# Delta-rule loop on one core: ACT copies the turned gated output ahead of squares and Relu, SP loads the value weights a slot ahead and the 16-blocks a slot later

## What is computed

```python
y = silu(causal_conv4(concat(q, k, v)))            # q, k: 16 heads, v: 32 heads
beta = sigmoid(b); g = -exp(A_log) * softplus(a + dt_bias)
q, k = l2norm(q) * DK ** -0.5, l2norm(k)
def step(S, inp):                                  # for every token
    S = S * exp(gt)[:, None, None]
    delta = (vt - einsum('hk,hkv->hv', kt, S)) * bt[:, None]
    S = S + kt[:, :, None] * delta[:, None, :]
    return S, einsum('hk,hkv->hv', qt, S)
gated = core * silu(z)
gated = gated * rsqrt(mean(gated * gated, -1) + EPS) * norm_w
out = gated.reshape(B, T, VDIM) @ W_out
```

## Time and profile before

| | |
|---|---|
| median of 3 runs | 3170.8 us (3170.05 to 3171.24) |
| the profiled execution | 3182.26 us |
| its span, first to last instruction | 3180.4 us |
| mean granted clock of TensorE | 0.974 of full speed |
| busy: PE, DVE, ACT, POOL | 92%, 71%, 62%, 48% |
| the loop's full part | about 380 to 2760 us, one slot 18.94 us |

### The profile page before, as it was taken

One profiled execution on the slowest core, in us unless ns is written; L12 is line 12 of the kernel. 1 busy time (PEld: TensorE's weight loads), 2 busy tenths in 40 slices (PEclk: granted clock), 3 DMA queues, 4 the chain that ended last, 5 costly groups with the idle time before them and its releaser, 6 DMA issues. The chain is left out here.

```text
span 3180.4 us, 70682 instructions
## 1 busy us (share of the span) xinstructions
PE 2911.2 (92%) x22765; PEld 2132.7 (67%) x22765; DVE 2258.0 (71%) x4805; ACT 1956.3 (62%) x6436; POOL 1520.6 (48%) x3616
## 2 busy tenths in 40 slices
PE   5998599999999999999999999999999999978998
PEld 4555377677767776777677767777777777764655
DVE  3432577777777777777777777777777777745766
ACT  4322577677767776777677767776777777633332
POOL 2000466656655565666666656665566666610000
PEclk8999799999999999999999999999999999978999
DMA  3001222222222222222222222222222222200000
GB/s 83 1 1 23 45 56 49 56 51 65 54 55 53 57 53 53 53 56 57 50 56 51 57 50 61 57 60 50 60 50 56 50 58 50 46 14 30 7 7 14
DMA packets 482417, 147.42 MB, mean 46 GB/s; under 512 B 352592, under 2 KB 481216, under 8 KB 482048
## 3 DMA queue, kind: packets, MB, share of 16 engines
q1 hardware_dynamic: 482048, 142.81, 20.7%
HBM read 97.40 MB, written 45.35 MB: 45 GB/s over the span
## 5 line engine op out<-in xcount | busy, mean ns | idle before, releaser
L920 ACT ACTIVATE raw<-bank 128x512 f32<-128x512 f32 x256 | 153.3, 599 | 388.0 <-PE bank L680 382.5
L748 PE MATMUL bank<-wout_h,gT 128*128 128x256 f32 x1024 | 258.4, 396 | 114.2 <-ACT gT L948 114.2
L475 POOL TENSOR_TENSOR Tb<-Tb,btmp 64x14 f32<-64x14 f32 (+6 forms) x896 | 281.4, 314 | 70.1
L748 PEld LDWEIGHTS bank<-wout_h,gT 128*128 128x128 f32 x1024 | 186.2, 192 | 184.7 <-ACT gT L948 164.1
L471 POOL TENSOR_TENSOR btmp<-Bk,Tb 64x14 f32<-64x14 f32 (+6 forms) x896 | 253.7, 283 | 65.6
L459 POOL TENSOR_SCALAR Tb<-Bk 64x256 f32<-64x256 f32 x64 | 70.8, 1106 | 447.1 <-issue 414.2
L680 PE MATMUL bank<-xnT,wv 128*128 128x512 f32 x512 | 259.5, 631 | 23.7 <-DMA cv<-in_L_attn_conv_w_dram 16.1
L1191 DVE SCALAR_TENSOR_TENSOR conv<-raw,ckq,conv 128x512 f32<-128x512 f32 x384 | 262.1, 751 | 20.7 <-ACT conv L921 18.7
L1191 DVE SCALAR_TENSOR_TENSOR conv<-raw,cv,conv 128x512 f32<-128x512 f32 x384 | 265.5, 757 | 7.4 <-ACT conv L921 5.4
L680 PE MATMUL bank<-xnT,wkq 128*128 128x512 f32 x512 | 254.3, 621 | 17.2 <-POOL mkX L376 7.2
L850 ACT ACTIVATE sq_kq<-bank 128x128 bf16<-128x128 f32 x512 | 134.7, 278 | 185.1 <-PE bank L633 185.1
(11 more groups left out here) (352 smaller groups left out, 7639.3 us busy)
## 6 DMA issues: line engine op xcount, KB each, us to landing
rowb<-decay_rows SPq DMA_DIRECT2D x128, 256.0 KB, 5.2
blk_n<-N SPq DMA_DIRECT2D x128, 256.0 KB, 2.9
Tp<-blk_t SPq DMA_DIRECT2D x128, 128.0 KB, 2.9
Wp<-blk_w SPq DMA_DIRECT2D x128, 128.0 KB, 3.1
wkq<-in_L_attn_W_qkvz_dram SPq DMA_DIRECT2D x32, 128.0 KB, 4.3
wv<-in_L_attn_W_qkvz_dram SPq DMA_DIRECT2D x16, 256.0 KB, 4.9
Bk<-blk_n SPq DMA_DIRECT2D x64, 64.0 KB, 2.7
blk_t<-Tb SPq DMA_DIRECT2D x64, 64.0 KB, 2.5
```

The lines of the kernel that those rows point to most:

```text
L475: pool.tensor_tensor(Tb[:, j + 1:, 0:j], Tb[:, j + 1:, 0:j], tmp, ALU.subtract).then_inc(row_rdy, 1)
L748: i = pe.matmul(bB[0][:, h], gT[:, 2 * h + v, :], wout[:, v, :], start=(v == 0), stop=(v == 1))
L920: act.activation(raw[h][:, j, :, 3:], bB[1 - j], ACT.Copy)
```

## The change

ACT: in `body` the three calls `clamp`, `squares`, `gtev` become `gtev`, `squares`, `clamp`.

SP: the load of wv and cv leaves `weights` for a function `value_weights`, which takes the step one ahead of the newest, so that it is issued in the slot of the head's chunk 0. The load of Bk leaves `dump` for `base_load`, which takes the step at S_F + 1, so it is issued in the slot behind the one in which N was stored. The body becomes `decays`, `weights`, `base_load`, `value_weights`, `base_out`, `dump`. Waits of the loads are the same; POOL, PE and DVE are unchanged.

```diff
-                    if t.c == 1 and not first:
-                        free = held(sp, t.at(1, -1))
-                        sp.wait_ge(m["made"], 2)
-                        wait(sp, y_rdy, free)
-                        h = bass.ds(t.head(), 1)
-                        sp.dma_start(wv[:], wq[:, :, h, 2 * P:4 * P]).then_inc(wv_in, 16)
-                        sp.dma_start(cv[:], cw[:, bass.ds(t.head(2, 2 * HK), 2), :]).then_inc(wv_in, 16)
...
+                def value_weights(s):
+
+
+                    t = s.back(S_P - 1)
+                    if not t.live or t.c != 1 or (t.i is None and t.off < C):
+                        return
+                    free = held(sp, t.at(1, -1))
+                    sp.wait_ge(m["made"], 2)
+                    wait(sp, y_rdy, free)
+                    h = bass.ds(t.head(), 1)
+                    sp.dma_start(wv[:], wq[:, :, h, 2 * P:4 * P]).then_inc(wv_in, 16)
+                    sp.dma_start(cv[:], cw[:, bass.ds(t.head(2, 2 * HK), 2), :]).then_inc(wv_in, 16)
...
-                    made, read, sent, free = (held(sp, v) for v in (t.done(), t.pairs(16), t.at(16, 16), t.pairs()))
+                    made, read = held(sp, t.done()), held(sp, t.pairs(16))
...
-                    if t.c % 2:
-                        sp.wait_ge(m["made"], 2)
-                        wait(sp, n_out, sent)
-                        wait(sp, base_rdy, free)
-                        sp.dma_start(Bk[:], blocks(nd)).then_inc(blk_in, 16)
+
+                def base_load(s):
+
+                    t = s.back(S_F + 1)
+                    if not t.live or t.c % 2 == 0:
+                        return
+                    sent, free = held(sp, t.at(16, 16)), held(sp, t.pairs())
+                    sp.wait_ge(m["made"], 2)
+                    wait(sp, n_out, sent)
+                    wait(sp, base_rdy, free)
+                    sp.dma_start(Bk[:], blocks(nd)).then_inc(blk_in, 16)
 
                 def body(s):
                     decays(s)
                     weights(s)
+                    base_load(s)
+                    value_weights(s)
                     base_out(s)
                     dump(s)
...
                     evac(s, 1)
+                    gtev(s)
+                    squares(s)
                     clamp(s)
-                    squares(s)
-                    gtev(s)
                     expo(s)
```

## The result

| | before | after |
|---|---|---|
| median | 3170.8 us (3170.1 to 3171.2, 4 runs) | 3644.8 us (3636.7 to 3651.1, 4 runs) |
| ratio to before | 1 | 1.149, 95% interval 1.147 to 1.152 |
| span of the profiled execution | 3180.4 us | 3634.8 us |
| mean granted clock of TensorE | 0.974 | 0.912 |

The change costs 474 us by the medians, 454 by the profiled executions. The forecast was 3699 us, with a range of 3540 to 3880. I read the waits of each engine first. The four blocks, one each for PE, POOL, ACT and DVE, show for the loop's full part (400 to 3200 us) after the change who waited for whom: total us, times, longest.

A forecast was written before the change was run, and what follows sets the result against it. The prediction took TensorE to bound the kernel; the moved Bk load's 527 us plus 33 at heads' starts less 32 for value weights gave +528, so 3182.3 + 528 − 11.5 = 3699 us, range 3540 to 3880.

The forecast's parts named there:

- What bounds: TensorE bounds the loop, 37.9 us a pair; POOL's wait for Bk is no slack, a 12.4 us chain follows it.
- The order on SP: Bk's load issues 0.8 us behind Exp's end, behind the row load; 2.2 us later in 15 pairs, +33 us.
- Landing: Bk's load behind the row load lands in 4.3 us (2.7 to 5.3); POOL starts 5.2 us behind Exp's end.
- POOL: POOL from Bk to L408's end: 12.36 us less 0.8 (0 to 1.5), ending 16.8 us behind Exp's end.
- The stop: TensorE idles some 8 us ahead of solve, which starts 14.7 us behind Exp's end; apply follows at 18.8.
- The way back: From B's apply to the next A's: 18.94 less 0.93 for gT plus 0.5 for the clock, 18.5 us.
- The value weights: Issuing wv and cv a slot earlier removes 16.1 us of TensorE waits and 1.55 in each of 10: −32 us.
- Sum: Whole kernel: 62 pairs at +8.5 us, 527, plus 33 at heads, less 32 for value weights: +528 us; 80%.
- That POOL's wait takes the later load in: Rival: POOL's 6.9 us idle ahead of L459 absorbs the later Bk load, both wins stay: 3027 us, 5%.
- That the stall is half as long: Rival: VectorE and ACT catch up more, half the excess, +4 us a pair: 3420 to 3540 us, 6%.
- That SP passes the row load: Rival: Bk's load moves less, as if SP could pass the row load; loss and gain cancel: 3171 us, 2%.
- That the half clock outlives its time: Rival: TensorE's half clock outlives its 5.2 us behind the stop, some 4 us more a pair: 3950 us, 7%.

The follow-up runs named there:

- section 2: The change with Bk's load ahead of the row load in SP's next slot body: 3089.2 us, ratio 0.975 to the kernel before.
- section 3: The change with Bk's load at its old place, weights ahead of the row load, squares ahead of gT: 3061.9 us, ratio 0.966 to before.

## Why the prediction was right, step by step

The direction, the place and the size held. By its own steps:

- **What bounds.** That POOL's idle time ahead of L459 is no slack, but a wait with a chain of 12.4 us without a hole behind it, is what decided. The load ahead of the row load, in section 2, shows it from one side, the waits for N in section 3 from the other.
- **The order on SP.** Bk's load was to stand 0.6 us behind the row load and 0.8 behind Exp's end. Measured 0.56 and 0.79. At a head's start the row load went out at 1909.13 and Bk's at 1911.96: 2.27 later than elsewhere, forecast 2.2. A to B was 1.9 us longer there, in the mean.

```profile
1909.13 0.37 SPq L297 DMA_DIRECT2D rowb<-decay_rows  x1
...
1911.96 0.59 SPq L363 DMA_DIRECT2D Bk<-blk_n  x1
```

- **Landing.** I took 4.3 from wkq's row and bounds of 2.7 and 5.3. The median is 4.7, and POOL started at +5.7 in place of +5.2. The row load landed 5.1 behind its issue, so 4.5 behind Bk's. The Trainium skill's rule of ring order (DMA: Bandwidth & Descriptors, Queues, rings and completion order) has Bk's completion come no sooner than that of the row load, on every DMA engine that both use: the trace agrees, 0.2 us behind it by the medians. The sum went by wkq's row, 4.3, and that was 0.4 short.
- **POOL.** From Bk to the end of L408 I had 11.6. It was 9.83 (1869.21 to 1879.04), so the step was mis-sized by 1.7. The chain no longer ran beside VectorE's convolution, and its instructions ran at their short times, as L456 (L442 before) 0.19 for 0.65 and L489 0.28 for 0.62 on the same 64x50. I took 0.8 off where 2.5 went, beyond my bound of 1.5, since I had counted the three long block rows (1.0) and not the scale's and the norms' instructions behind them (1.5).
- **The stop.** Solve was to come 14.7 us behind Exp's end; it came at 14.0. TensorE's part from there to apply took 3.93 us (forecast 3.7) and was the later of the two, not VectorE's: Us ended 0.5 us before. Exp's end to apply: 17.9, forecast 18.8.
- **The way back.** B to the next A was to be 18.5 and was 18.26, but by errors that offset each other. The stop for gT was worth more than its 0.93. TensorE before, and after:

```profile
1617.26 1.89 PE L696 MATMUL bank<-wz_h,xnT 128*128 128x256 f32 x8
```

```profile
1886.81 1.89 PE L710 MATMUL bank<-wz_h,xnT 128*128 128x256 f32 x8
1888.53 1.89 PE L762 MATMUL bank<-wout_h,gT 128*128 128x256 f32 x8
```

  From the z projection's start to L748 it was 2.82 us, to L762 it is 1.72, so 1.10 went, and 0.09 more in these matmuls themselves (1.82 to the next start, now 1.73). Against it, TensorE waits 0.33 for Xs, since ACT stands 0.48 us for TensorE's transposes ahead of gT, and all that follows on ACT is late by it. I had counted that hole only towards Exp, not towards what TensorE waits for in the next slot. And of the 0.5 for the clock 0.2 came (apply 1.27 for 1.06): the half clock lasted 4.3 us into the work, not 5.2.
- **The value weights.** −32 forecast, −15 measured alone. The mis-sized term is this price, which I took from one execution.
- **Sum.** 62 × 7.5 + 33 − 15 = 483, against 474 measured and 528 forecast. The forecast's excess is the pair, 46.4 for 45.4, less the 17 of the value weights. In the pair, POOL took 1.7 less and the way back 0.25 less, Bk's start came 0.5 later, and from L408 to apply it took 2.4 in place of 2.0. The long stretch shows in 60 pairs, not 62, and the heads' starts cost 29 us in place of 33 (15 × 1.9): together 19 us less, more than the 9 by which 483 is too high; what makes up for it stays open.

**The rivals.** That POOL's wait takes the later load in fell: POOL started on Bk 14.9 us behind A's apply, where it was 2.8 before, and `out_scale` stood behind it. That the stall is half as long fell: a pair grew by 7.5 of the 8.5. That SP passes the row load fell. That the half clock outlives its time held in a small way in the kernel with the load alone, where apply ran at it.

What would have changed my reading was TensorE's stop under 5 us; it was 7.05 here, 6.7 in the mean, forecast about 8.

## What to carry to other kernels

An engine that works in order pays for every wait ahead of an instruction. When a load moves past another one, look up what that other one waits for, and when this comes: here it was 9 us later (1611.85 and 1620.77), while the load's own condition had long been met. Idle time ahead of an instruction is slack only where its follow-up has a gap too; take the distance from the end of the chain to its first reader before calling an engine free.

And when one edit of three loses, the other two may still pay. Time them apart.

## What the runs showed of the hardware

- POOL's instructions ran at two speeds within one kernel: 0.28 and 0.62 us for the same subtraction of 64x50, 1.03 and 1.41 for the same power of 128x4 (1874.33 and 1890.52 in the trace of after). What decides is which of VectorE's instructions runs beside. In the trace of before this one lies over POOL's instructions from 1619 to the end of L448, the 0.62 and 0.65 of the earlier trace rows among them:

```profile
1618.10 4.21 DVE L1191 SCALAR_TENSOR_TENSOR conv<-raw,cv,conv 128x512 f32<-128x512 f32 x6
```

  Its inputs are all tiles that the kernel keeps in SBUF. The 51 subtractions of 64x50 that met only it in the whole trace took 0.61 in the median; the 57 beside Us, Wk or S, each of which reads a PSUM bank (`bank`, the output of TensorE's rows), took 0.28, as did those beside nothing. In the chain from Bk to L408 seven instructions were long before, six of them beside L1191, and their excess is the 2.5 us by which the chain got shorter: the late load moved it out from beside the convolution. That is a reading of when the long ones stand; no run took the convolution away by itself.
- A stop of 7.05 us costs TensorE a granted clock of 0.50 (1.2 GHz) for over 4 us of work behind it. Stretches of 2 us, after the change (PE, PEld, DVE, ACT, POOL busy, PEclk, DMA share, GB/s):

```profile
1876.00:1878.00 2.00, 0.50 (x2) 0.54 (x3) 0.00 (x0) 1.33 (x5) 1.92 (x3) 0.50 0.00 0
1878.00:1880.00 2.00, 2.00 (x18) 1.78 (x18) 0.78 (x3) 0.74 (x2) 1.69 (x8) 0.50 0.00 0
1880.00:1882.00 2.00, 2.00 (x20) 1.88 (x17) 1.27 (x4) 0.76 (x3) 1.53 (x7) 0.54 0.00 0
1882.00:1884.00 2.00, 2.00 (x17) 1.76 (x16) 1.27 (x5) 1.93 (x8) 1.55 (x6) 1.00 0.00 0
```

It stretched 2.09 us of work to 3.93, and still filling the stop gave back only 15 us of 474 (25 inside the loop): at the full clock TensorE waits 1.18 us for Us instead.
